# A graph attention kernel: ten of sixteen blocks per tile turned by DMA, the adjacency loaded in quarters

## The chip, the cores and the metric

One Trainium2 chip, one of its cores. The time is device microseconds for one execution of the whole program. TensorE is written PE, VectorE DVE, ScalarE ACT, GpSimd POOL, SyncE SP.

## What is computed

```python
h = jnp.maximum(_layernorm(x, axis=-1), 0.0)              # x: 8192 x 128, fp32
scores = jnp.einsum('nd,md->nm', h, ks)                   # ks: 8192 x 128, fp32
scores = leaky_relu(scores, negative_slope=0.2)
scores = jnp.where(adj > 0, scores, NEG_BIG)              # adj: 8192 x 8192, int32
attn = softmax(scores, axis=1)
out = x + jnp.einsum('nm,md->nd', attn, ks)
```

## The kernel before

The rows of x are taken in 64 tiles of 128. For a tile, its 8192 keys are worked in 16 blocks of 512 columns; two blocks are a pair, and two pairs (2048 columns) are a load of the adjacency.

- PE makes a block's scores from three fp16 products of 512 columns (h and the keys are each split in a high and a low half).
- DVE makes a mask from a load of the adjacency (L578), and adds it to a pair's scores (L596), which go from PSUM to SBUF with their running minimum. L611 takes the tile's minimum, once per tile.
- ACT does the leaky step (L458) and the exponentials (L467), a pair at a time, in place.
- The output product needs the probabilities transposed, 128 keys to the partition, in a high and a low fp16 half. There are two ways. A block of `BY_PE` is transposed by PE in fp32 (L376, four transposes) into PSUM; ACT then writes the high half (L475) and DVE the low half (L605). A block of `BY_DMA` is split first, by POOL (`split_half`: CAST at L317, subtraction at L319), and then both halves are turned at once by a DMA transpose (`turn`, L254, "turned block").
- PE adds either kind into the output with eight products per block (L391, L392).

Room for turned blocks: six slots for the halves (`R_SLOTS`), eight for the turned ones (`D_SLOTS`), both carved out of the buffer `keys_in` after the keys are done with. In the trace both appear as `keys_in`.

The order of all work is written out by hand. `steps` runs one step per tile, each of 16 slots `j`, and every engine's program has its own loop over these slots. In step i, PE makes the scores of tile i+1 while the rest works on tile i. A lag says how many slots after the block's own number a piece stands: `behind(i, j, lag, kind, ...)` gives the block of slot j - lag, if it is of that kind. On PE a turned block is added ten slots behind its number (`ADD_LAG`), a block of PE's own is transposed four and added six slots behind.

SP issues all DMAs in one queue, in the order of the program: a load of x and a store of the output for every four tiles, the adjacency loads (`load_adj`), and the turns. A turn waits for its split (`half_lo_ready`), so what stands behind it on SP waits too. A load waits until the mask that last read its slot is made (`mask_ready`). POOL's split waits for the exponentials and until the halves' slot was turned (`turned_in`, six turned blocks back). DVE's L596 waits until the pair of twelve pairs ago was transposed or split.

Of the kernel before, what the change touches and what calls it, by code (L numbers as in the profile page):

```python
# [5 lines left out]
def gat_kernel(nc: bass.Bass, x: bass.AP, adj: bass.AP, ks: bass.AP, out: bass.AP):  # L6
# [18 lines left out]
    PER_PAIR = PAIR // P  # L25
    LOAD = 2 * PAIR
    LOADS = M // LOAD
    SLOTS = 4
    ADJ_SLOTS = 4
    RING = 12  # L30
# [5 lines left out]
    EXP_LAG = 2  # L36
    T_LAG = 4
    OUT_LAG = 6
    LO_LAG = 3
    TURN_LAG = 5  # L40
    ADD_LAG = 10

    BY_DMA = tuple(b for b in range(BLOCKS) if b % 2 == 1 or b in (12,))
    BY_PE = tuple(b for b in range(BLOCKS) if b not in BY_DMA)

    EPS = 1e-5
# [10 lines left out]
    with ExitStack() as ctx:  # L57
# [6 lines left out]
        def sem(name):  # L64
            return ctx.enter_context(nc.semaphore(name))
# [49 lines left out]
        ps_out = psum("ps_out", [P, 2, BLOCK], fp32)  # L115


        adj_loaded = [sem(f"adj_loaded{s}") for s in range(2 * ADJ_SLOTS)]
        keys_loaded = [sem(f"keys_loaded{p}") for p in range(PAIRS)]
        x_loaded = [sem(f"x_loaded{s}") for s in range(2)]  # L120
        stored = sem("stored")
# [50 lines left out]
        def cols(b):  # L172
            return slice(b * BLOCK, (b + 1) * BLOCK)
# [54 lines left out]
        def _(sp):  # L228
# [8 lines left out]
                sp.wait_ge(out_ready, (g + 1) * GROUP)  # L237
                sp.dma_start(out_groups[g], out_tile[:, g % 2, :, :]).then_inc(stored, 16)

            def load_adj(q, p):  # L240
                n = q * PAIRS + p
                if n >= 2 * ADJ_SLOTS:
                    sp.wait_ge(mask_ready, n // 2 - ADJ_SLOTS + 1)
                sp.dma_start(adj_in[:, n // 2 % ADJ_SLOTS, n % 2 * PAIR:(n % 2 + 1) * PAIR],
                             adj_tiles[q // GROUP, q % GROUP, :, p * PAIR:(p + 1) * PAIR]).then_inc(adj_loaded[n % (2 * ADJ_SLOTS)], 16)

            def turn(t, b):
                n = nth_dma(t, b)
# [9 lines left out]
            for p in range(PAIRS):  # L258
                c = slice(p * PER_PAIR, (p + 1) * PER_PAIR)
                sp.dma_start(keys_in[:, c, :], key_chunks[:, c, :]).then_inc(keys_loaded[p], 16)  # L260
            for p in range(6):
                load_adj(0, p)
            load_x(1)

            def step(i, odd, more, this, prev, ahead):
                for j in range(BLOCKS):
                    if j % 2 == 1:
                        q, p = divmod((i + 1) * PAIRS + j // 2 + 6, PAIRS)
                        if q < TILES:
                            load_adj(q, p)  # L270
                    for b in (0, 1):
                        turning = behind(i, j, TURN_LAG - b, BY_DMA, this, prev) if j % 2 == 1 else None
                        if turning:
                            turn(*turning)
                    if j == 11 and prev and i % GROUP == 0:
                        store(i // GROUP - 1)
                        if i // GROUP + 1 < GROUPS:
                            load_x(i // GROUP + 1)
# [5 lines left out]
        def _(pool):  # L284
# [38 lines left out]

            def step(i, odd, more, this, prev, ahead):
                for j in range(BLOCKS):
                    for b in (0, 1):
                        split = behind(i, j, LO_LAG - b, BY_DMA, this, prev) if j % 2 == 1 else None
                        if split:
                            split_half(*split)
                    if j == 7 and ahead:  # L330
                        normalise(i + 2)

# [173 lines left out]
        def _(dve):  # L506
# [64 lines left out]
            def make_mask(q, k):  # L571

                n = q * LOADS + k
                dve.wait_ge(adj_loaded[2 * (n % ADJ_SLOTS)], (n // ADJ_SLOTS + 1) * 16)
                dve.wait_ge(adj_loaded[2 * (n % ADJ_SLOTS) + 1], (n // ADJ_SLOTS + 1) * 16)
                if q > 0 or k >= 2:
                    dve.wait_ge(masked_ready, q * PAIRS + 2 * k - 2)
                nc.vector.tensor_scalar(mask[:, k % 2, :], adj_in[:, n % ADJ_SLOTS, :], 0, MASKED, ALU.is_le, ALU.mult) \  # L578
                    .then_inc(mask_ready, 1)
# [125 lines left out]
```

## Time and profile before

| | |
|---|---|
| median of three runs | 1605.21 us (1602.86 to 1609.5) |
| the profiled execution's own time | 1603.36 us, span of its instructions 1601.6 us |
| granted TensorE clock | 0.996 |
| PE busy | 1561.6 us, 98% of the span |
| DVE, ACT, POOL busy | 89%, 84%, 83% |
| DMA | 434.52 MB, 271 GB/s over the span |

A line of the page or of an answer gives an engine, a source line, an operation, and its output and inputs by name, so `keys_in<-scores` at L317 is the split into the halves. "Busy" is time in which the engine has an instruction under way; PE's matmuls overlap, and their ends are modelled. SP has no busy time of its own: its rows (SPq) are the issue of a DMA, and a row's duration holds what the issue waited for as well. "To landing" is from the start of the issue until all of the DMA's completion signals are in.

### The profile page before, as it was taken

What the parts mean: (1) busy time and instruction counts of PE and PEld (TensorE: products, weight loads), DVE (VectorE), ACT (ScalarE), POOL (GpSimd) and SP (SyncE); (2) the same over time, 40 slices, a digit from 0 to 9 for tenths busy, and PEclk for the clock granted to TensorE, in tenths of its full rate; (3) what the DMA queues carried; (4) which work ended last, traced back from release to release, by engine and by line L of the source; (5) the groups of instructions that cost most, each with busy time, mean ns of one, the idle gap of its engine ahead of it and who ended that gap; (6) DMA issues with size and microseconds to landing.
All of it is one profiled execution on the core that took longest, in us unless ns stands there. A gap on an engine that the chain in (4) does not pass through costs nothing.

```text
span 1601.6 us, 37520 instructions
## 1 busy us (share of the span) xinstructions
PE 1561.6 (98%) x13186; PEld 1155.7 (72%) x13186; DVE 1423.2 (89%) x2528; ACT 1350.2 (84%) x2017; POOL 1332.6 (83%) x1352
## 2 busy tenths in 40 slices
PE   5699999999999999999999999999999999999998
PEld 3377777777777777777777777777777777777776
DVE  6998998998998998998898998899899899898895
ACT  6688888888888888888888888888888888888886
POOL 1588888888888888888888888888888888888887
PEclk9999999999999999999999999999999999999999
DMA  8699999999999999999999999999999999999996
GB/s 275 176 251 273 275 280 283 283 286 271 285 272 276 270 281 286 278 269 276 287 279 294 271 286 275 282 266 281 272 276 284 278 287 281 287 283 283 270 267 119
DMA packets 695098, 434.52 MB, mean 271 GB/s; under 512 B 617088, under 2 KB 625280, under 8 KB 694912
## 3 DMA queue, kind: packets, MB, share of 16 engines
q1 hardware_dynamic: 694912, 432.12, 111.2%
q8 instruction: 107, 1.75, 0.5%
q14 instruction: 79, 0.65, 0.1%
HBM read 276.82 MB, written 4.19 MB: 175 GB/s over the span
## 4 chain that ended last, share of the span: by engine, by line
PE 93%; DMA 1%; DVE 1%; POOL 1%; ACT 0%; issue 0%; POOLq 0%; DVEq 0%; ACTq 0%
PE ps_out L391 27%; PE ps_out L392 14%; PE ps_scores L365 13%; PE ps_scores L367 13%; PE ps_scores L366 13%; PE ps_T L376 12%; DMA keys_in<-keys_in 1%; PE ps_out L343 0%; PE ps_out L390 0%; POOL keys_in L319 0%; ACT scores L467 0%; DVE mask L578 0%; PE ps_out L389 0%; POOL keys_in L317 0%; DVE keys L567 0%
## 5 line engine op out<-in xcount | busy, mean ns | idle before, releaser
L319 POOL TENSOR_TENSOR keys_in<-scores,keys_in 128x512 f16<-128x512 f32 x576 | 728.8, 1265 | 46.5
L596 DVE CUSTOM_DVE_ANT_0 scores<-ps_scores,mask,minus_scale 128x1024 f32<-128x1024 f32 x512 | 653.8, 1277 | 17.0 <-PE ps_scores L367 2.1
L458 ACT ACTIVATE scores<-scores 128x1024 f32<-128x1024 f32 x512 | 537.6, 1050 | 79.5 <-DVE pair_min L596 79.5
L317 POOL CAST keys_in<-scores 128x512 f16<-128x512 f32 x576 | 463.7, 805 | 164.4 <-ACT scores L467 160.0
L467 ACT ACTIVATE scores<-scores,neg_max 128x1024 f32<-128x1024 f32 x512 | 583.1, 1139 | 0.0
L391 PE MATMUL ps_out<-keys,keys_in 128*128 128x256 f16 x2240 | 431.4, 273 | 1.1 <-DMA keys_in<-keys_in 1.1
L605 DVE TENSOR_TENSOR probsT_lo<-ps_T,probsT_hi 128x512 f16<-128x512 f32 x448 | 308.3, 688 | 126.9 <-ACT probsT_hi L475 118.1
L365 PE MATMUL ps_scores<-keysT_hi,hT_hi 128*128 128x512 f16 x1024 | 389.6, 381 | 17.2 <-DVE keysT_lo L560 10.6
L392 PE MATMUL ps_out<-keys,keys_in 128*128 128x128 f16 x2240 | 400.8, 219 | 0.0
L475 ACT ACTIVATE probsT_hi<-ps_T 128x512 f16<-128x512 f32 x448 | 264.7, 591 | 151.2 <-PE ps_T L376 146.8
L366 PE MATMUL ps_scores<-keysT_lo,hT_hi 128*128 128x512 f16 x1024 | 389.6, 380 | 0.0
L367 PE MATMUL ps_scores<-keysT_hi,hT_lo 128*128 128x512 f16 x1024 | 389.5, 380 | 0.0
L391 PE MATMUL ps_out<-keys,probsT_hi 128*128 128x256 f16 x1792 | 345.0, 273 | 8.2 <-issue 5.5
L578 DVE TENSOR_SCALAR mask<-adj_in 128x2048 bf16<-128x2048 int32 x256 | 326.1, 1274 | 0.0
L392 PE MATMUL ps_out<-keys,probsT_lo 128*128 128x128 f16 x1792 | 320.9, 220 | 0.0
L376 PEld LDWEIGHTS ps_T<-ident,scores 128*128 128x128 f32 x1792 | 224.1, 141 | 85.5 <-ACT scores L467 1.0
L391 PEld LDWEIGHTS ps_out<-keys,keys_in 128*128 128x128 f16 x2240 | 219.0, 98 | 81.0 <-DMA keys_in<-keys_in 2.6
L376 PE MATMUL ps_T<-ident,scores 128*128 128x128 f32 x1792 | 269.4, 273 | 0.5 <-ACT scores L467 0.5
L392 PEld LDWEIGHTS ps_out<-keys,keys_in 128*128 128x128 f16 x2240 | 219.0, 98 | 58.5
L391 PEld LDWEIGHTS ps_out<-keys,probsT_hi 128*128 128x128 f16 x1792 | 175.5, 98 | 32.8 <-issue 6.8
L367 PEld LDWEIGHTS ps_scores<-keysT_hi,hT_lo 128*128 128x128 f16 x1024 | 100.4, 98 | 121.7 <-issue 1.4
L392 PEld LDWEIGHTS ps_out<-keys,probsT_lo 128*128 128x128 f16 x1792 | 175.5, 98 | 11.5
(52 smaller groups left out, 829.5 us busy)
## 6 DMA issues: line engine op xcount, KB each, us to landing
adj_in<-in_adj_dram SPq DMA_DIRECT2D x512, 512.0 KB, 5.3
keys_in<-keys_in SPq DMA_TRANSPOSE x576, 5.5
x_in<-in_x_dram SPq DMA_DIRECT2D x16, 256.0 KB, 4.3
keys_in<-in_L_gnn_ks_dram SPq DMA_DIRECT2D x8, 512.0 KB, 7.4
out_dram<-out_tile SPq DMA_DIRECT2D x16, 256.0 KB, 3.8
```

What stands on the lines that cost most here:

```text
L317: nc.gpsimd.tensor_copy(half[:, 0:BLOCK], probs(t, b)).then_inc(half_hi_ready, 1)
L319: nc.gpsimd.tensor_tensor(half[:, BLOCK:2 * BLOCK], probs(t, b), half[:, 0:BLOCK], ALU.subtract) \
L365: nc.tensor.matmul(dst, hT_hi[:, odd, :], keysT_hi[:, cols(b)], start=True, stop=False)
L366: nc.tensor.matmul(dst, hT_hi[:, odd, :], keysT_lo[:, cols(b)], start=False, stop=False)
L367: nc.tensor.matmul(dst, hT_lo[:, odd, :], keysT_hi[:, cols(b)], start=False, stop=True) \
L376: mm = nc.tensor.transpose(ps_T[:, n % 2, k * P:(k + 1) * P], probs(t, b)[:, k * P:(k + 1) * P], ident[:, :])
L391: nc.tensor.matmul(o[:, 0:2 * D], hi_part, keys[:, c, :], start=(b == FIRST and k == 0), stop=False)
L392: return nc.tensor.matmul(o[:, D:2 * D], lo_part, keys[:, c, D:2 * D], start=False, stop=False)
L458: nc.scalar.activation(s, s, ACT.Prelu, alpha=1.0 / SLOPE).then_inc(leaky_ready, 1)
L467: nc.scalar.activation(s, s, ACT.Exp, bias=neg_max[:, t % 2:t % 2 + 1], scale=-SLOPE, accum_out=pair_sum[:, t % 2, p:p + 1]).then_inc(prob ...
L578: nc.vector.tensor_scalar(mask[:, k % 2, :], adj_in[:, n % ADJ_SLOTS, :], 0, MASKED, ALU.is_le, ALU.mult) \
L596: nc.vector.tensor_tensor_reduce(out=score_pair(q, p), in0=ps_scores[:, slots, :].rearrange("p s k -> p (s k)"), in1=mask[:, (p // 2) % 2, ...
```

## The change

Block 4 joins the blocks turned by DMA, so there are ten of them in a tile (1, 3, 4, 5, 7, 9, 11, 12, 13, 15) and six transposed by PE. The adjacency is loaded 512 columns (256 KB) at a time in place of 1024 (512 KB), one load in every slot in place of one in every second slot; a mask still covers 2048 columns, and waits for four loads. The splits and turns stood in odd slots only, up to two in a slot; now each stands in the slot of its own block number plus 2 (`LO_LAG`) and plus 4 (`TURN_LAG`), at most one in a slot.

```diff
     LOADS = M // LOAD
+    PER_LOAD = LOAD // BLOCK
...
-    LO_LAG = 3
-    TURN_LAG = 5
+    LO_LAG = 2
+    TURN_LAG = 4
     ADD_LAG = 10
 
-    BY_DMA = tuple(b for b in range(BLOCKS) if b % 2 == 1 or b in (12,))
+    BY_DMA = tuple(b for b in range(BLOCKS) if b % 2 == 1 or b in (4, 12))
...
-            def load_adj(q, p):
-                n = q * PAIRS + p
-                if n >= 2 * ADJ_SLOTS:
-                    sp.wait_ge(mask_ready, n // 2 - ADJ_SLOTS + 1)
-                sp.dma_start(adj_in[:, n // 2 % ADJ_SLOTS, n % 2 * PAIR:(n % 2 + 1) * PAIR],
-                             adj_tiles[q // GROUP, q % GROUP, :, p * PAIR:(p + 1) * PAIR]).then_inc(adj_loaded[n % (2 * ADJ_SLOTS)], 16)
+            def load_adj(q, b):
+                n = q * BLOCKS + b
+                if n >= PER_LOAD * ADJ_SLOTS:
+                    sp.wait_ge(mask_ready, n // PER_LOAD - ADJ_SLOTS + 1)
+                sp.dma_start(adj_in[:, n // PER_LOAD % ADJ_SLOTS, n % PER_LOAD * BLOCK:(n % PER_LOAD + 1) * BLOCK],
+                             adj_tiles[q // GROUP, q % GROUP, :, cols(b)]) \
+                    .then_inc(adj_loaded[n % (PER_LOAD * ADJ_SLOTS)], 16)
...
-            for p in range(6):
-                load_adj(0, p)
+            for b in range(12):
+                load_adj(0, b)
...
                 for j in range(BLOCKS):
-                    if j % 2 == 1:
-                        q, p = divmod((i + 1) * PAIRS + j // 2 + 6, PAIRS)
-                        if q < TILES:
-                            load_adj(q, p)
-                    for b in (0, 1):
-                        turning = behind(i, j, TURN_LAG - b, BY_DMA, this, prev) if j % 2 == 1 else None
-                        if turning:
-                            turn(*turning)
+                    q, b = divmod((i + 1) * BLOCKS + j + 11, BLOCKS)
+                    if q < TILES and (i, j) > (-1, 0):
+                        load_adj(q, b)
+                    turning = behind(i, j, TURN_LAG, BY_DMA, this, prev)
+                    if turning:
+                        turn(*turning)
...
                 for j in range(BLOCKS):
-                    for b in (0, 1):
-                        split = behind(i, j, LO_LAG - b, BY_DMA, this, prev) if j % 2 == 1 else None
-                        if split:
-                            split_half(*split)
+                    split = behind(i, j, LO_LAG, BY_DMA, this, prev)
+                    if split:
+                        split_half(*split)
...
-                dve.wait_ge(adj_loaded[2 * (n % ADJ_SLOTS)], (n // ADJ_SLOTS + 1) * 16)
-                dve.wait_ge(adj_loaded[2 * (n % ADJ_SLOTS) + 1], (n // ADJ_SLOTS + 1) * 16)
+                for s in range(PER_LOAD):
+                    dve.wait_ge(adj_loaded[PER_LOAD * (n % ADJ_SLOTS) + s], (n // ADJ_SLOTS + 1) * 16)
```

SP's queue before, in the middle of the program (a turn is a DMA_TRANSPOSE; its two halves are 8 x 128 columns):

```order
312 L254 DMA_TRANSPOSE keys_in<-keys_in 128x8x128
313 L244 DMA adj_in<-in_adj_dram 128x1024
314 L254 DMA_TRANSPOSE keys_in<-keys_in 128x8x128 x2
315 L244 DMA adj_in<-in_adj_dram 128x1024
316 L254 DMA_TRANSPOSE keys_in<-keys_in 128x8x128
```

SP's queue after the change, over a little more than half a tile:

```order
404 L256 DMA_TRANSPOSE keys_in<-keys_in 128x8x128
405 L245 DMA adj_in<-in_adj_dram 128x512 x2
406 L256 DMA_TRANSPOSE keys_in<-keys_in 128x8x128
407 L245 DMA adj_in<-in_adj_dram 128x512
408 L256 DMA_TRANSPOSE keys_in<-keys_in 128x8x128
409 L245 DMA adj_in<-in_adj_dram 128x512
410 L256 DMA_TRANSPOSE keys_in<-keys_in 128x8x128
411 L245 DMA adj_in<-in_adj_dram 128x512 x2
```

Where each turn had one load between it and the next, and two turns stood together once in a tile, there are now two loads of half the size at six places of a tile and one at four; no two turns stand together.

PE's order before, in slot 8, from the three products of a score block on (`ps_T` is the transpose's PSUM buffer, `ps_out` the output's):

```order
1551 L365 MATMUL ps_scores<-keysT_hi,hT_hi 128x512
1552 L366 MATMUL ps_scores<-keysT_lo,hT_hi 128x512
1553 L367 MATMUL ps_scores<-keysT_hi,hT_lo 128x512
1554 L376 MATMUL ps_T<-ident,scores 128x128 x4
1555 L391 MATMUL ps_out<-keys,probsT_hi 128x256
```

And after, in the same slot (its lines stand one higher in the file):

```order
1543 L364 MATMUL ps_scores<-keysT_hi,hT_hi 128x512
1544 L365 MATMUL ps_scores<-keysT_lo,hT_hi 128x512
1545 L366 MATMUL ps_scores<-keysT_hi,hT_lo 128x512
1546 L390 MATMUL ps_out<-keys,probsT_hi 128x256
1547 L391 MATMUL ps_out<-keys,probsT_lo 128x128
```

The four transposes of block 4 are gone; its output products move from slot 10 to slot 14, among those of the turned blocks.

## Rows read from the trace of the kernel before

**Rows 1.** The page's first part, busy time by engine

```profile
PE 1561.6 (98%) x13186; PEld 1155.7 (72%) x13186; DVE 1423.2 (89%) x2528; ACT 1350.2 (84%) x2017; POOL 1332.6 (83%) x1352
```

**Rows 2.** The page's chain that ended last, shares by engine and by line

```profile
PE 93%; DMA 1%; DVE 1%; POOL 1%; ACT 0%; issue 0%; POOLq 0%; DVEq 0%; ACTq 0%
PE ps_out L391 27%; PE ps_out L392 14%; PE ps_scores L365 13%; PE ps_scores L367 13%; PE ps_scores L366 13%; PE ps_T L376 12%; DMA keys_in<-keys_in 1%; PE ps_out L343 0%; PE ps_out L390 0%; POOL keys_in L319 0%; ACT scores L467 0%; DVE mask L578 0%; PE ps_out L389 0%; POOL keys_in L317 0%; DVE keys L567 0%
```

**Rows 3.** Timeline of DVE, 780 to 833: start us, us, instruction

```profile
781.71 0.16 DVE L611 TENSOR_REDUCE row_min<-pair_min 128x1 f32<-128x8 f32 x1
...
805.85 0.16 DVE L611 TENSOR_REDUCE row_min<-pair_min 128x1 f32<-128x8 f32 x1
```

**Rows 4.** Windows: stretch, its us, busy us (instructions) by engine, PEclk, DMA share, GB/s

```profile
779.97:804.06 24.09, 24.09 (x206) 17.90 (x205) 21.67 (x40) 20.66 (x32) 20.76 (x22) 1.00 1.15 285
18.00:24.00 6.00, 1.58 (x10) 1.16 (x10) 4.66 (x12) 3.71 (x6) 0.00 (x0) 0.80 1.03 411
```

**Rows 5.** The chain from 801 to 802.2: start us, us, what

```profile
801.64 0.44 PE ps_T L376 x4
```

**Rows 6.** Timeline of POOL, 780 to 833

```profile
782.12 0.61 POOL L317 CAST keys_in<-scores 128x512 f16<-128x512 f32 x1
782.81 1.18 POOL L319 TENSOR_TENSOR keys_in<-scores,keys_in 128x512 f16<-128x512 f32 x1
783.96 0.61 POOL L317 CAST keys_in<-scores 128x512 f16<-128x512 f32 x1
```

**Rows 7.** Waits of POOL, 781.9 to 806: us in total, times, longest

```profile
POOL keys_in L317 <- ACT scores L467: 2.2, 3, 1.2
```

**Rows 8.** Timeline of all engines, 803 to 804

```profile
803.35 1.26 DVE L578 TENSOR_SCALAR mask<-adj_in 128x2048 bf16<-128x2048 int32 x1
...
803.48 1.60 POOL L317 CAST keys_in<-scores 128x512 f16<-128x512 f32 x1
```

**Rows 9.** Lines L254 and L244: duration ns min/median/max, first and last start

```profile
L254 SPq DMA_TRANSPOSE keys_in<-keys_in x576: 1231/1677/3927, 63.0 to 1594.4; - x192
...
DMA to landing us min/median/max: 3.0/5.5/8.8
...
L244 SPq DMA_DIRECT2D adj_in<-in_adj_dram x512: 328/572/2006, 13.0 to 1555.0; - x171
...
DMA to landing us min/median/max: 3.6/5.3/11.2
```

**Rows 10.** Timeline of SP, 438 to 460

```profile
446.43 1.23 SPq L254 DMA_TRANSPOSE keys_in<-keys_in  x1
447.71 0.57 SPq L244 DMA_DIRECT2D adj_in<-in_adj_dram  x1
448.38 1.57 SPq L254 DMA_TRANSPOSE keys_in<-keys_in  x1
...
453.52 2.87 SPq L254 DMA_TRANSPOSE keys_in<-keys_in  x1
```

**Rows 11.** Timeline of SP, 262 to 272

```profile
267.55 0.57 SPq L238 DMA_DIRECT2D out_dram<-out_tile  x1
268.17 0.42 SPq L234 DMA_DIRECT2D x_in<-in_x_dram  x1
268.64 0.45 SPq L244 DMA_DIRECT2D adj_in<-in_adj_dram  x1
```

**Rows 12.** Waits of SP: us in total, times, longest

```profile
SPq L254 <- POOL keys_in L319: 443.0, 371, 3.5
SPq L244 <- DVE mask L578: 47.2, 52, 9.3
```

**Rows 13.** Groups of POOL by line: xcount, busy us, mean ns, idle before

```profile
L305 POOL TENSOR_SCALAR x_norm<-x_in,mean_var,rstd 128x128 f32<-128x128 f32 x64 | 103.4, 1616 | 6.7
L300 POOL TENSOR_TENSOR rstd<-var_eps,minus_half 128x1 f32<-128x1 f32 x64 | 36.1, 564 | 5.3
L297 POOL TENSOR_SCALAR var_eps<-mean_var 128x1 f32<-128x1 f32 x64 | 14.1, 220 | 38.2 <-DVE mean_var L513 32.8
```

More of the change, by code:

```diff
@@ L115, in gat_kernel @@
         ps_out = psum("ps_out", [P, 2, BLOCK], fp32)
-        adj_loaded = [sem(f"adj_loaded{s}") for s in range(2 * ADJ_SLOTS)]
+        adj_loaded = [sem(f"adj_loaded{s}") for s in range(PER_LOAD * ADJ_SLOTS)]
         keys_loaded = [sem(f"keys_loaded{p}") for p in range(PAIRS)]
```

## The prediction

> **What bounds the kernel now.** The engine totals come first: PE is busy for 1561.6 of 1601.6 us [rows 1], which by itself proves little. The chain that ended last says more: 93% of it is PE: products for the output 41% of the span, the three products of a score block 39%, the fp32 transposes (L376) 12% [rows 2]. One line per tile, the reduction at L611, gives the beat: it runs at 781.71 and at 805.85, 24.1 us apart [rows 3]; 64 such beats are 1542 us, and the rest of the span is start and end. In one beat PE is busy for 24.09 of 24.09 us [rows 4]. So PE alone sets the time, and PE time taken out of a beat comes out of the span, as long as the others keep the shorter beat. How near they are to that is the question of this case.
>
> **PE.** One more block turned by DMA takes four transposes of L376 out of each tile. On the chain they hold 0.44 us together [rows 5]. Its twelve score products and eight output products stay. New PE beat: 24.1 - 0.44 = 23.65 us. Over 64 tiles that would be 28 us. ACT and DVE each lose one block's piece and are idle for 10 to 14% of the beat [rows 1, 4]; nothing is due from them.
>
> **POOL.** It gets a tenth split per tile. Starts follow each other as 782.12, 782.81, 783.96 [rows 6]: 0.69 and 1.15, so 1.84 us for a block. In the beat shown POOL waits 2.2 us for the exponentials of ACT and for nothing else that is listed [rows 7], so its work, short gaps included, is 24.1 - 2.2 = 21.9 us, and 21.9 + 1.84 = 23.7 us after. That is the new PE beat and no less. The masks are in this already: the CAST at 803.48 takes 1.60 us and not 0.61, because the mask at L578 (1.26 us from 803.35) runs beside it [rows 8]. POOL can hold 23.7, but no longer catches up after anything.
>
> **SP.** This is the term I trust most and it goes the wrong way. SP is one queue that issues loads and turns in order, and an issue takes its sequencer time. A turn takes 1231 ns at least, and a load that follows a turn 572 ns at the median [rows 9]. With the short gaps between starts (446.43, 447.71, 448.38) a turn holds SP for 1.28 and the load behind it for 0.67 us [rows 10]. What does a load of half the bytes cost? A store of 256 KB behind a turn took 0.57 us (at 267.55), the same as a 512 KB load behind a turn, and the x load and the adjacency load behind it 0.42 and 0.45 us [rows 11]. So an issue's price is not in its bytes: a quarter load behind a turn costs 0.67 us, and one behind another load some 0.50 (0.45 and the gap, as from 268.17 to 268.64 and on).
> - Before: nine turns and eight loads, 9 x 1.28 + 8 x 0.67 = 16.9 us, with the store and the x load of every fourth tile (about 1 us in four) 17.1 us of 24.1.
> - After: ten turns, ten loads behind a turn and six behind a load (the order of the built program: double loads at six places, single ones at four). 10 x 1.28 + 10 x 0.67 + 6 x 0.50 + 0.25 = 22.75 us.
> So the floor of SP rises by 5.6 us, from 71% of the beat to 96% of the new one.
>
> That floor is without push-back. The turns' median is 1677 ns, 0.45 above their least [rows 9]. Only part of it is waiting for a split: 371 of 576 turns waited for one, and 205 did not [rows 12]; turns of 1.57 and 2.87 us stand beside ones of 1.23 [rows 10]. So a turn is also held until the DMA queue takes it. At what rate is the queue asked? SP's floor before offered 786 KB (a load and a turn) per 1.95 us, 400 GB/s, where the DMA engines moved 285 [rows 4] in a mix, and 411 in a stretch of loads alone [rows 4]. After, SP's floor offers 16 x 262 + 10 x 262 KB = 6.8 MB in 22.75 us, 300 GB/s. The queue is asked much less hard, so less push-back is due; not none, since 300 is still above the mean moved now. Bounds: 0 and 0.45 us per turn. I take 0.18, two fifths of what the median turn has now, since the asked rate comes down most of the way to the moved one. Ten turns: 1.8 us. **SP's beat: 22.75 + 1.8 = 24.5 us**, and that is above the 24.1 of today: (24.5 - 24.1) x 64 = +26 us.
>
> What hid SP until now: 443 us in total of waiting for the split, 47 us for a mask to free its slot [rows 12], 7.7 us per tile. The change spends 5.6 us of it, the shorter beat 0.45, and what is left must cover the push-back.
>
> Late next: a turned block has six slots, about 9 us, from its turn's place to its output products; a turn lands 5.5 us after its issue at the median, 8.8 at most [rows 9]. About 3.5 us are to spare, so single late turns cost nothing, but a queue slower than the beat uses that up within a few tiles and then PE waits at L391 for the turned block in every tile. Queued behind a late turn on SP are the adjacency loads; these are issued eleven blocks ahead and land 5.3 us after issue, so DVE's masks stay fed.
>
> **Bytes and the DMA engines.** The turned bytes grow from 9 x 262 to 10 x 262 KB per tile, the adjacency stays 4.2 MB: 6.55 to 6.8 MB, in 23.65 us 288 GB/s against 285 now [rows 4]. The pieces of the loads shrink from 4096 to 2048 bytes; x loads have such pieces, and no row shows them alone. If they moved at the 411 GB/s of the larger ones, the DMA engines would have room; a loss of a few per cent of rate would not.
> The Trainium skill (DMA: Bandwidth & Descriptors, Rules for kernel authors) asks for at least 1 MiB per DMA for most of the bandwidth, which speaks against cutting 512 KB loads in two. Its fit in the same page (2.0 us and the bytes at 436 GB/s per DMA) would give 16 x 2.6 = 42 us of loads per tile if they went one at a time. Here three or so are under way at once: a load lands 5.3 us after its issue [rows 9], and 17 DMAs start in 24.1 us, one per 1.4 us. So by the rows I price the smaller size at nothing beyond the issue.
>
> **The start.** Twelve issues instead of six before x's second load: 6 x 0.48 us behind a queue that is already filled with the keys; nothing.
>
> **Rivals.**
> - *SP keeps up; PE or POOL sets the beat.* If push-back falls to under 0.1 us per turn, SP needs under 23.7 us and the beat is 23.65 to 23.7: -0.4 x 64 = -26 to -28 us, 1577 to 1580. For it: the asked rate falls by a quarter, and the change spreads turns to at most one per slot where one slot had two. Against: the margin is 0.9 us per tile, POOL has none, and a turn waits for its split in order, so SP can't use its free moments ahead of time. Chance 0.25. The Trainium skill (DMA: Bandwidth & Descriptors, Issuing engines are not separate DMA queues) calls the sequencer's time to initiate a DMA usually small relative to the DMA itself; by that rule eight more issues would not count and this rival would be the forecast. Here the issue of a turn has at least 1.23 us against 3.0 to land at the least [rows 9], so it does count.
> - *Both effects cancel*, SP's beat at 24.0 to 24.2: 1598 to 1612. Chance 0.17.
> - *SP-bound as worked out*, 24.2 to 25.3: 1613 to 1682. Chance 0.48.
> - *Push-back stays as it is or POOL's lateness joins in.* At 0.36 to 0.45 us per turn SP's beat is 26.4 to 27.2 us: +2.3 to +3.1 x 64, 1750 to 1800. Or POOL's run of three splits in a row (blocks 3, 4, 5 and 11, 12, 13) with the normalisation behind block 5 (0.22 + 0.56 + 1.62 us, [rows 13]), 3 x 1.84 + 2.4 = 7.9 us in three slots of 1.5, makes the splits late by some 2 us and eats the turn's spare time. Chance 0.10 together.
> That the change doesn't do what it says is excluded by the order of the built program.
>
> **The numbers.** Sum against the profiled execution's own time, 1603.4: 1603.4 + 26 = 1629; the median of the runs shown stands 0.1% higher, so 1631. The range takes in PE's beat at the low end and an SP beat of 25.3 at the high end: 1577 to 1680. The likeliest case's own range is 1613 to 1680. A measurement of this kernel can tell about 0.5% from no change: faster than 1597 0.25, within 0.17, slower than 1613 0.58.
>
> **What the changed profile would show.** L611 24.4 to 24.6 us apart; L376 x1536; turns x640 and loads x1024 of 256 KB; SP's wait for POOL L319 down from 443 us to under 100; PE or its weight loads waiting at the turned L391 for the DMA, some 50 us where they now have under 4; loads' issue at 0.57 and 0.45 us as before. Wrong would be: the beat at 23.65 with SP still waiting over 100 us for splits (push-back gone), a quarter load's issue clearly under 0.45, or PE held by DVE's L596, which waits for splits that POOL finishes late.

## The result, and the profile after

The changed kernel takes 1665.81 us (median of 4 runs, 1658.7 to 1671.5) against 1604.03 us before (median of 4, 1602.62 to 1609.5): a ratio of 1.0381, 95% interval 1.0365 to 1.0397. That is 62 us slower; the forecast was 26. The profiled execution has a span of 1664.7 us and a granted clock of 0.998, so TensorE's clock has no part in it.

The page's first part after the change, busy time by engine, and its chain that ended last, by engine (beside [rows 1, 2]):

```profile
PE 1554.4 (93%) x12930; PEld 1112.0 (67%) x12930; DVE 1417.7 (85%) x2464; ACT 1329.6 (80%) x1953; POOL 1436.7 (86%) x1480
...
POOL 26%; PE 16%; DMA 14%; ACT 7%; DVE 7%; issue 6%; SPq 4%; POOLq 0%; DVEq 0%; ACTq 0%
```

PE was 93% of the chain and is 16% of it. Its place is taken by what the view reads as a loop: split on POOL, turn by DMA, product on PE. Whether POOL belongs in it is looked at below.

Three beats in the windows view (columns as in [rows 4]), from one row minimum at 763.31 to the third behind it at 837.92:

```profile
763.31:837.92 74.61, 70.97 (x601) 51.46 (x599) 65.11 (x115) 60.67 (x91) 66.58 (x69) 1.00 1.17 277
```

The same for three beats of the kernel before:

```profile
781.71:854.10 72.39, 72.39 (x617) 53.80 (x616) 65.23 (x118) 62.06 (x94) 62.41 (x64) 1.00 1.15 288
```

PE has less work (23.66 us a beat against 24.13) and now idles 1.2 us a beat; the beat is 24.87 here. Over the whole run the row minimum, this time by its line, with durations in ns and the first and last start:

```profile
L610 DVE TENSOR_REDUCE row_min<-pair_min x64: 160/161/163, 51.2 to 1637.3; 128x1 f32<-128x8 f32 x64
```

(1637.3 - 51.2) / 63 = 25.18 us a beat. Before it is (1575.6 - 50.5) / 63 = 24.21 us, from the same view of that kernel. The difference, 0.97 x 63 = 61 us, is the whole loss: it lies in the steady state, not at the ends.

What PE waits for, and what SP waits for, from the two views of waits (us in total, times, longest):

```profile
PE ps_out L390 <- DMA keys_in<-keys_in: 67.0, 93, 2.2
...
SPq L256 <- POOL keys_in L319: 261.5, 306, 3.7
```

PE's products of turned blocks (now L390) wait 67 us for the DMA. The weight loads of the same line wait 145 us. These overlap, and neither was over 4 us before. SP's listed wait for splits went from 443 us [rows 12] to 261.5. That looks as if SP still had four microseconds a beat to spare, and it had none, as its timeline shows over one beat (start us, us, instruction; x2 joins two issues in one row):

```profile
805.58 1.24 SPq L256 DMA_TRANSPOSE keys_in<-keys_in  x1
806.87 1.77 SPq L245 DMA_DIRECT2D adj_in<-in_adj_dram  x2
808.73 1.24 SPq L256 DMA_TRANSPOSE keys_in<-keys_in  x1
810.01 1.07 SPq L245 DMA_DIRECT2D adj_in<-in_adj_dram  x2
811.19 1.24 SPq L256 DMA_TRANSPOSE keys_in<-keys_in  x1
812.47 1.38 SPq L245 DMA_DIRECT2D adj_in<-in_adj_dram  x2
813.95 1.24 SPq L256 DMA_TRANSPOSE keys_in<-keys_in  x1
815.23 0.58 SPq L245 DMA_DIRECT2D adj_in<-in_adj_dram  x1
815.91 1.44 SPq L256 DMA_TRANSPOSE keys_in<-keys_in  x1
817.40 0.58 SPq L245 DMA_DIRECT2D adj_in<-in_adj_dram  x1
818.07 1.24 SPq L256 DMA_TRANSPOSE keys_in<-keys_in  x1
819.36 1.06 SPq L245 DMA_DIRECT2D adj_in<-in_adj_dram  x2
820.51 1.24 SPq L256 DMA_TRANSPOSE keys_in<-keys_in  x1
821.80 1.89 SPq L245 DMA_DIRECT2D adj_in<-in_adj_dram  x2
823.78 1.24 SPq L256 DMA_TRANSPOSE keys_in<-keys_in  x1
825.06 1.06 SPq L245 DMA_DIRECT2D adj_in<-in_adj_dram  x2
826.22 1.90 SPq L256 DMA_TRANSPOSE keys_in<-keys_in  x1
828.17 0.58 SPq L245 DMA_DIRECT2D adj_in<-in_adj_dram  x1
828.85 1.37 SPq L256 DMA_TRANSPOSE keys_in<-keys_in  x1
830.26 0.58 SPq L245 DMA_DIRECT2D adj_in<-in_adj_dram  x1
830.94 1.24 SPq L256 DMA_TRANSPOSE keys_in<-keys_in  x1
```

Ten turns from 805.58 to 830.94, 25.36 us, with no gap over 0.12 us. Turns that are taken at once cost 1.24, a pair of loads 1.06, a single load 0.58. At these prices the beat would be 12.4 + 6 x 1.06 + 4 x 0.58 + 1.4 of gaps = 22.5 us. What is over that is holding: 1.0 us on the turns (815.91, 826.22, 828.85), 1.9 us on pairs of loads (806.87, 812.47, 821.80).

Where is the wait for splits in this? POOL's subtractions, each the end of a split, from the same stretch:

```profile
819.66 1.17 POOL L319 TENSOR_TENSOR keys_in<-scores,keys_in 128x512 f16<-128x512 f32 x1
821.46 1.16 POOL L319 TENSOR_TENSOR keys_in<-scores,keys_in 128x512 f16<-128x512 f32 x1
823.25 1.16 POOL L319 TENSOR_TENSOR keys_in<-scores,keys_in 128x512 f16<-128x512 f32 x1
```

Splits and turns are made in the same order, so the n-th of one belongs to the n-th of the other. By that count these are the splits of blocks 3, 4 and 5, whose turns start at 826.22, 828.85 and 830.94: each split had been ready for 5.4 to 6.5 us. Counted so for all turns, none starts before its own split has ended, in either kernel. So a wait for a split stands in the gap ahead of a turn's row and not in the row's duration, and what a turn's row has over its least is holding. SP was in truth idle for its own split for 79.8 us before the change (118 turns) and for 6.2 us after (11 turns, all in the last 31 us), where the view lists 443.0 and 261.5: it puts down any stretch in which some later split's signal came. The same count over 56 tiles (from the fifth row minimum to the 61st), in us a beat:

| | before | after | `nine_quarter` | `ten_half` | `ten_whole` | `ten_quarter_hi` |
|---|---|---|---|---|---|---|
| beat | 24.10 | 25.16 | 24.14 | 25.91 | 27.43 | 24.24 |
| turns at their least | 11.08 | 12.31 | 11.08 | 12.26 | 12.31 | 11.91 |
| holding on turns | 5.67 | 1.51 | 2.00 | 6.78 | 11.21 | 1.08 |
| loads, x and stores | 5.06 | 9.51 | 9.08 | 5.40 | 2.70 | 9.07 |
| gaps | 2.26 | 1.82 | 1.99 | 1.45 | 1.23 | 2.18 |
| of these, waiting for the turn's own split | 0.90 | 0.00 | 0.24 | 0.00 | 0.00 | 0.42 |

(The four kernels on the right belong to the experiments below.) Before the change SP waited for splits 0.9 us a beat; a tenth turn needs 1.28 of issue alone.

### The profile page after: what moved, and what is told of

The parts are those of the page before. It is cut to its first block, busy times and chain, and to the rows that moved or that the text cites. A ratio compares the mean times of both kernels' runs of the same rounds, so it can differ in the third digit from the quotient of the medians.

```text
span 1664.7 us, 37777 instructions
## 1 busy us (share of the span) xinstructions
PE 1554.4 (93%) x12930; PEld 1112.0 (67%) x12930; DVE 1417.7 (85%) x2464; ACT 1329.6 (80%) x1953; POOL 1436.7 (86%) x1480
## 4 chain that ended last, share of the span: by engine, by line
POOL 26%; PE 16%; DMA 14%; ACT 7%; DVE 7%; issue 6%; SPq 4%; POOLq 0%; DVEq 0%; ACTq 0%
DMA keys_in<-keys_in 14%; POOL keys_in L319 14%; POOL keys_in L317 9%; PE ps_out L390 5%; ACT scores L466 4%; DVE mask L577 3%; DVE scores L595 2%; ACT scores L457 2%; PE ps_out L391 2%; PE ps_scores L366 2%; PE ps_scores L365 2%; PE ps_scores L364 2%; PE ps_T L375 2%; POOL var_eps L297 2%; SPq L256 2%
## 5 line engine op out<-in xcount | busy, mean ns | idle before, releaser
L319 POOL TENSOR_TENSOR keys_in<-scores,keys_in 128x512 f16<-128x512 f32 x640 | 795.3, 1243 | 51.6
L317 POOL CAST keys_in<-scores 128x512 f16<-128x512 f32 x640 | 511.6, 799 | 118.5 <-ACT scores L466 117.2
L390 PE MATMUL ps_out<-keys,keys_in 128*128 128x256 f16 x2496 | 482.0, 273 | 68.6 <-DMA keys_in<-keys_in 67.0
L391 PE MATMUL ps_out<-keys,keys_in 128*128 128x128 f16 x2496 | 446.3, 219 | 0.0
L604 DVE TENSOR_TENSOR probsT_lo<-ps_T,probsT_hi 128x512 f16<-128x512 f32 x384 | 263.6, 686 | 175.5 <-ACT probsT_hi L474 174.6
L390 PEld LDWEIGHTS ps_out<-keys,keys_in 128*128 128x128 f16 x2496 | 243.7, 98 | 206.2 <-DMA keys_in<-keys_in 145.4
L577 DVE TENSOR_SCALAR mask<-adj_in 128x2048 bf16<-128x2048 int32 x256 | 364.4, 1424 | 0.1
L390 PE MATMUL ps_out<-keys,probsT_hi 128*128 128x256 f16 x1536 | 294.7, 273 | 9.4 <-issue 6.5
L391 PE MATMUL ps_out<-keys,probsT_lo 128*128 128x128 f16 x1536 | 274.1, 219 | 0.0
L391 PEld LDWEIGHTS ps_out<-keys,keys_in 128*128 128x128 f16 x2496 | 244.3, 98 | 38.5
L375 PE MATMUL ps_T<-ident,scores 128*128 128x128 f32 x1536 | 230.5, 273 | 0.5 <-ACT scores L466 0.5
L390 PEld LDWEIGHTS ps_out<-keys,probsT_hi 128*128 128x128 f16 x1536 | 150.2, 98 | 40.0 <-issue 9.4
```

What stands on the lines that cost most here:

```text
L317: nc.gpsimd.tensor_copy(half[:, 0:BLOCK], probs(t, b)).then_inc(half_hi_ready, 1)
L319: nc.gpsimd.tensor_tensor(half[:, BLOCK:2 * BLOCK], probs(t, b), half[:, 0:BLOCK], ALU.subtract) \
L375: mm = nc.tensor.transpose(ps_T[:, n % 2, k * P:(k + 1) * P], probs(t, b)[:, k * P:(k + 1) * P], ident[:, :])
L390: nc.tensor.matmul(o[:, 0:2 * D], hi_part, keys[:, c, :], start=(b == FIRST and k == 0), stop=False)
L391: return nc.tensor.matmul(o[:, D:2 * D], lo_part, keys[:, c, D:2 * D], start=False, stop=False)
```

## The experiments

Seventeen kernels ran, in the groups below. Unless said otherwise a ratio is against the kernel before, whose own median beside them was 1603.3 to 1604.0 us.

**Which part of the change costs.** `ten_half` is the changed kernel with the old 512 KB loads:

```diff
-                    q, b = divmod((i + 1) * BLOCKS + j + 11, BLOCKS)
-                    if q < TILES and (i, j) > (-1, 0):
-                        load_adj(q, b)
+                    if j % 2 == 1:
+                        q, p = divmod((i + 1) * PAIRS + j // 2 + 6, PAIRS)
+                        if q < TILES:
+                            load_adj(q, p)
```

> The changed kernel (ten turned blocks, one per slot) with the adjacency again in loads of 1024 columns, eight per tile. Theory A (SP's queue: issues plus the time a DMA is held fill 25.1 us of every beat): eight issues fewer take 8 x 0.55 = 4.4 us off SP's floor of 22.75, so SP is no longer full by issues, and the beat falls to between 23.7 (POOL) and 24.1: 1577 to 1605 us. Theory B (the tenth split on POOL sets the beat, the chain shows POOL first): the split is still there, so the time stays within 1% of 1666. Theory C (the 2048-byte pieces move more slowly): as A.

1710.68 us, ratio 1.0665 (1.0638 to 1.0693): slower than the change itself, as neither theory had it.

`nine_quarter` is the kernel before with quarter loads, placed as the change places them.

> The kernel before (nine turned blocks, its lags) with the adjacency in quarter loads, one per slot: the other half of the change alone. Theory A: SP's floor is 9 x 1.28 + 9 x 0.67 + 7 x 0.50 + 0.25 = 21.3 us, with the 2.4 us of holding seen after the change 23.7, just under PE's 24.1: 1603 to 1620 us. Theory B: as before, 1600 to 1608. Theory C: clearly slower than before, towards 1640 to 1665, since all the small pieces are there.

1605.08 us, 1.0005 (0.9995 to 1.0015): eight more issues a tile and pieces of 2,048 bytes cost the time of nine blocks nothing. SP pays 4.0 us a beat more for loads and gets 3.7 back in holding on turns (the table above).

`nine_cut32` cuts each 512 KB load of the kernel before into 992 and 32 columns, sixteen issues a tile. Half of the issues have pieces of 3,968 bytes, the other half of 128.

> The kernel before with each 1024-column load issued as two, one of 992 and one of 32 columns: eight issues more per tile, the same bytes, nearly all in pieces of 3968 bytes. Theory A: SP's floor rises from 17.1 to 21.1 us and what a turn is held stays near the 5.7 us per beat of before, so SP needs more than 24.1: 1620 to 1700 us. Theories B and C (the number of issues costs nothing): 1600 to 1610.

1616.99 us, 1.0071 (1.0048 to 1.0095). That is 13 us, between the two forecasts, and the even split in `nine_quarter` doesn't have it. Whether the issues or the 128-byte pieces cost it wasn't tested.

`nine_half_lags` takes the new lags alone, and `ten_half_oldlags` block 4 alone (`b in (4, 12)`, nothing else changed).

> The kernel before with the new lags alone (block 12's split and turn in slots of their own). All theories: PE's beat stays, 1600 to 1610 us.

> The kernel before with block 4 turned by DMA and nothing else changed: split and turn of block 4 stand with those of block 5 in one slot, as 12 and 13 do. Theory D: the queue has the same ten turns and eight loads as in ten_half, 1690 to 1730 us. If spreading the turns over the slots is what helps or harms, it differs from 1711 by more than 1%. Theory B: 1650 to 1720.

1603.37 us, 0.9997 (0.9988 to 1.0006), and 1699.61 us, 1.0588 (1.0568 to 1.0609). So the tenth turned block is the whole loss and more, +96 us. Both results lie where the queue's theory put them; the range of POOL's holds the second too. The lags cost nothing with nine blocks and 11 us with ten and 512 KB loads (1710.68 against 1699.61). The quarter loads, which my sum made the culprit, give 45 us back (1710.68 to 1665.81).

**What a turn waits for.** SP's timeline in `ten_half`, and behind it three single turns of that kernel by their line (duration ns; start; landing is counted from the start of the issue):

```profile
782.97 2.24 SPq L255 DMA_TRANSPOSE keys_in<-keys_in  x1
...
785.95 4.95 SPq L255 DMA_TRANSPOSE keys_in<-keys_in  x2
...
797.55 1.47 SPq L255 DMA_TRANSPOSE keys_in<-keys_in  x1
...
799.77 5.60 SPq L255 DMA_TRANSPOSE keys_in<-keys_in  x2
```

```profile
L255 SPq DMA_TRANSPOSE keys_in<-keys_in x1: 2238/2238/2238, 783.0 to 783.0; - x1
DMA to landing us min/median/max: 6.9/6.9/6.9
...
L255 SPq DMA_TRANSPOSE keys_in<-keys_in x1: 2902/2902/2902, 785.9 to 785.9; - x1
...
L255 SPq DMA_TRANSPOSE keys_in<-keys_in x1: 1465/1465/1465, 797.5 to 797.5; - x1
DMA to landing us min/median/max: 6.6/6.6/6.6
...
L255 SPq DMA_TRANSPOSE keys_in<-keys_in x1: 3462/3462/3462, 799.8 to 799.8; - x1
```

The turn of 782.97 lands at 789.9; the issue of the next one, from 785.95, is held for 2.90 us and ends at 788.85, 1.0 us before that. The turn of 797.55 lands at 804.15; the next one's issue ends at 799.77 + 3.46 = 803.23, 0.9 us before. The same in the changed kernel:

```profile
L256 SPq DMA_TRANSPOSE keys_in<-keys_in x1: 1237/1237/1237, 823.8 to 823.8; - x1
DMA to landing us min/median/max: 5.2/5.2/5.2
...
L256 SPq DMA_TRANSPOSE keys_in<-keys_in x1: 1902/1902/1902, 826.2 to 826.2; - x1
```

823.78 + 5.2 = 828.98, and the issue of the turn behind it ends at 826.22 + 1.90 = 828.12, 0.9 us before. These three are the common case, not a rule. Of the turns held by over 0.2 us with their split ready, 330 of 451 in `ten_half` end their issue 0.8 to 1.2 us before the turn ahead lands, and 71 of 112 in the changed kernel; but the turn of 782.97 above, held for 1.0 us, was let go 2.5 us before the one ahead of it landed, and in `ten_quarter_hi` (below) only 15 of 76 are in that band. Where turns are held, then, they mostly follow the landing of the turn ahead, and what stands in front of a turn counts: with 512 KB loads a turn lands in 5.4 us at the median, with quarter loads in 4.2 (the lines' own views).

**Size of the loads.** `ten_third` cuts each 2,048 columns into 688, 680 and 680, `ten_mixed` into 1,024, 512 and 512, both with twelve loads a tile in the same slots; `ten_whole` has 1 MB loads on SP.

```diff
-    PER_LOAD = LOAD // BLOCK
+    PER_LOAD = 3
+    CUTS = (0, 688, 1368, 2048)
```

> The changed kernel with three loads per mask (688, 680, 680 columns), twelve per tile, placed so that a turn mostly has one load ahead of it, twice two. Theory D: SP's issues need 10 x 1.28 + 10 x 0.67 + 2 x 0.50 + 0.25 = 20.75 us, and a turn behind one 350 KB load is held to about 0.15 us less than its issues take, so holding stays rare, 2.5 to 3.5 us per beat: 23.3 to 24.3, which POOL and PE keep at 23.7 or more: 1580 to 1615 us. That would be level with or faster than the kernel before. Theory B (POOL): 1650 to 1680.

> As ten_third, same twelve issues in the same places, but a mask's loads are 1024, 512 and 512 columns. If only the number of issues counts, the same time as ten_third within 0.5%. Theory D: the turns behind a 1024-column load (four per tile) are held 0.7 us or so more than there, the others a little less: 1.5 to 2.5 us per beat more, 1.5 to 8% over ten_third.

> Ten turned blocks, adjacency in whole loads of 2048 columns (1 MB, four per tile) on SP. Theory D (what the first four runs left: SP's queue is full in every kernel with ten blocks; a turn costs SP either its issue or, if that is longer, the time until about 1 us before the turn ahead of it has landed, and each load in between delays that landing by its bytes): SP's issues alone need 10 x 1.28 + 4 x 0.67 + 0.25 = 15.7 us, but four of the ten turns stand behind 1 MB, so they are held about 4 us each and the other six 1.3 to 2.3: 24 to 30 us, 1600 to 1960, most likely 1690 to 1760. Theory A as first put (issues alone): 1577 to 1605. Theory B (POOL's tenth split): 1650 to 1680, as after.

1657.67 us, 1.0346 (1.0321 to 1.0372); 1675.2 us, 1.0442 (1.0426 to 1.0457); 1806.3 us, 1.1263 (1.1246 to 1.128). The first missed what I expected by far: thirds are only 8 us better than quarters, and the intervals of the two ratios overlap. The second is 1.1% over the first, outside both forecasts (within 0.5%, and 1.5 to 8%). The third is slower than its likeliest range and inside the wide one. The size of the largest load matters at a fixed number of issues (1,024 columns against 688: 17.5 us), and below a third of 1 MB smaller loads give nothing more.

`ten_whole_act` moves 1 MB loads to ACT's queue so that they don't stand between turns, and `nine_whole_act` does so to the kernel before.

```diff
+                    if j % 4 == 1:
+                        n = ((i + 1) * BLOCKS + j + 11) * PARTS // 4
+                        if n < PARTS * LOADS * TILES:
+                            issue_adj(act, n)
```

> Ten turned blocks, whole loads, but issued by ACT's queue, so SP holds nothing but turns, x and stores. Theory D: no load stands between two turns in SP's queue, SP needs 12.8 us of issues; if a load on ACT's queue doesn't push a turn's landing far back, the beat falls to POOL's or PE's 23.7: 1575 to 1600 us, faster than both kernels. Theory B: 1650 to 1680, since POOL does the same splits. A turn that lands late because of the shared DMA engines would leave it above 1610 and show as PE waiting for the turned block.

> The kernel before with whole loads issued by ACT: the control for the issue on ACT. All theories: PE's beat of 24.1 stays, 1600 to 1610 us. Slower would show what four issues of 0.45 us per tile cost on ACT.

The first takes 2073 to 2210 us in four executions. The second takes 2060 to 2119; its ratio, of the two shortest, is 1.2883 (1.2839 to 1.2928), 462 us. Both missed by some 400 us or more, with granted clocks of 0.85 to 0.91. What four issues on ACT cost was thus not learnt; they themselves take 0.33 to 0.40 us each. SP is held: its issue of a turn takes up to 17.3 us and the slowest turn lands after 28.6. The DMA issues and the waits for turned blocks of `nine_whole_act`, from an execution of 2118.6 us:

```profile
adj_in<-in_adj_dram ACTq DMA_DIRECT2D x253, 1024.0 KB, 6.6
keys_in<-keys_in SPq DMA_TRANSPOSE x576, 6.6
...
PEld ps_out L395 <- DMA keys_in<-keys_in: 426.9, 105, 13.2
PE ps_out L395 <- DMA keys_in<-keys_in: 375.8, 96, 12.7
```

A turn lands in 6.6 us at the median and PE waits up to 13 us for one. Why a load that starts on another queue delays a turn so much was not settled.
The Trainium skill (DMA: Bandwidth & Descriptors, Issuing engines are not separate DMA queues) says that DMAs of all engines interleave on the same 16 DMA engines whoever issues them, and that a second issuer saves sequencer time alone; the trace agrees that nothing was won, and the loss of 462 us is more than the page leads one to expect.

**The queue taken off the path.** `ten_quarter_halfbytes` halves the bytes of each adjacency load after the first sixteen, so half the adjacency is stale. `ten_quarter_hi` turns only the high half of each block after the first eight; the low halves are stale.

```diff
-                sp.dma_start(turned[:, n % D_SLOTS, :, :], halves[:, n % R_SLOTS, :], transpose=True) \
+                k, w = (2 * PER_BLOCK, SLOT) if n < D_SLOTS else (PER_BLOCK, BLOCK)
+                sp.dma_start(turned[:, n % D_SLOTS, 0:k, :], halves[:, n % R_SLOTS, 0:w], transpose=True) \
```

> The changed kernel, in which every adjacency load after the first sixteen brings 256 of its 512 columns (the other half of the mask is left from earlier tiles): the same issues, half the adjacency's bytes. Theory A in its two parts: if the holding (2.4 us per beat) is the DMA engines' doing, it mostly goes, SP needs 22.8 to 23.5 and the beat is POOL's 23.7, 1575 to 1590 us; if it is the issue itself, nothing changes, 1655 to 1670. Theory B: within 1% of 1666. Theory C: much faster, since fewer bytes are moved, 1580 to 1610.

> The changed kernel, in which every turn after the first eight turns only the high halves (512 of 1024 columns; the low halves in the products are stale): the same number of issues and loads, half the turned bytes. Theory D: if a turn's issue goes by its size, 1.23 falls to 0.6 to 0.8 us and its landing comes earlier, SP needs 17 to 19 us, and the beat is POOL's or PE's 23.7: 1575 to 1590 us. If an issue has a price of its own whatever it moves, as the loads' has, SP stays at 22.75 plus less holding: 1600 to 1650. Theory B: 1650 to 1680.

1628.03 us, 1.0149 (1.0133 to 1.0164), and 1611.71 us, 1.0048 (1.0035 to 1.0062). Number and order of the issues are those of the change. The first result lies between all the forecasts for it, the second in that of an issue price that doesn't go by bytes. The turn's line in `ten_quarter_hi`:

```profile
L257 SPq DMA_TRANSPOSE keys_in<-keys_in x640: 1188/1195/2708, 62.9 to 1603.2; - x160
...
DMA to landing us min/median/max: 2.4/3.4/6.0
```

Half the bytes cost the same issue (1,195 ns against 1,237) and land in 3.4 us instead of 4.2. PE then waits 1.9 us in all for turned blocks, and 54 of the 62 us are gone. The issue time of SP, 22.5 us less 10 x 0.04, was never the bound by itself.

A rival to the queue stays open: the 16 DMA engines behind it. The page gives the time of the queue's packets as a share of the engines' span (packets, MB, share), after the change:

```profile
q1 hardware_dynamic: 836224, 448.94, 112.9%
```

It is 111.2% before, 100.6% in `ten_quarter_halfbytes` and 95.6% in `ten_quarter_hi`; counted over the middle of the run, 16 packets or more are under way for 94% of the time before, 95% after, and 65% in each of the two. The changed kernel moves 16.8 MB more than the one before, both at 271 GB/s, and 16.8 MB at that rate are 62 us. Bytes alone can't be the bound, since the same 451 MB take 1657.7 us in thirds and 1806.3 as whole loads (273 and 250 GB/s). But both kernels with half the bytes relieve the queue and the engines at once, and no run here relieves one without the other.

**The 28 us that didn't come.** PE's work is 0.44 us a beat shorter, yet `ten_quarter_hi` is 8 us slower than before. Its beat, and what PE waits for in it:

```profile
785.30:809.55 24.25, 23.81 (x204) 17.41 (x202) 22.81 (x39) 20.18 (x31) 22.47 (x24) 1.00 0.99 231
```

```profile
PE ps_out L391 <- DVE probsT_lo L605: 27.6, 63, 0.8
```

63 waits, one a tile, of 0.44 us: as much as the change saved. One step back, DVE's timeline around that wait and POOL's beside it:

```profile
801.47 2.13 DVE L578 TENSOR_SCALAR mask<-adj_in 128x2048 bf16<-128x2048 int32 x1
803.53 0.68 DVE L605 TENSOR_TENSOR probsT_lo<-ps_T,probsT_hi 128x512 f16<-128x512 f32 x1
```

```profile
801.36 1.16 POOL L320 TENSOR_TENSOR keys_in<-scores,keys_in 128x512 f16<-128x512 f32 x1
802.47 1.61 POOL L318 CAST keys_in<-scores 128x512 f16<-128x512 f32 x1
```

The mask takes 2.13 us where 1.22 is its least. It starts 0.11 us into a subtraction that runs to 802.52 and ends at 803.60, 1.08 us after it. The CAST behind the subtraction takes 1.61 us instead of 0.61 and ends at 804.08, 0.48 us after the mask. Each waits for the other. The probsT_lo behind the mask is late for PE.
The Trainium skill (SBUF — State Buffer, Who interferes with whom) calls the port pair that VectorE and GpSimd share "an exclusive lock" that a tensor_scalar can take and for which the later one blocks; these rows agree, in both directions.

Three kernels on top of `ten_quarter_hi` and one control test this. `ten_hi_halfmask` makes each mask of half its columns, `ten_hi_halfsplit` takes the difference in each split over half its columns, `ten_hi_halfbytes` halves the load bytes, and `nine_hi` is `nine_quarter` with high halves alone. Of these the first leaves half of each mask stale, the second a part of the low halves that no turn reads.

```diff
-                nc.gpsimd.tensor_tensor(half[:, BLOCK:2 * BLOCK], probs(t, b), half[:, 0:BLOCK], ALU.subtract) \
+                w = BLOCK if n < R_SLOTS else BLOCK // 2
+                nc.gpsimd.tensor_tensor(half[:, BLOCK:BLOCK + w], probs(t, b)[:, 0:w], half[:, 0:w], ALU.subtract) \
```

> The kernel that turns only high halves of ten blocks (1611.7 us), and each mask made of 1,024 of its 2,048 columns after the first two, so that its other half is stale and the output is not the reference's. Theory P (VectorE and GpSimd hold each other up: masks of 1,728 ns mean beside GpSimd's splits make probsT_lo late by 0.43 us a tile, and GpSimd is 98% taken): masks of 700 to 950 ns, splits that wait less for them, no wait of TensorE at the output products; 1,577 to 1,592 us. Rival Q (what is left of the loss is still the DMA queue or TensorE's own instructions): unchanged at 1,607 to 1,615 us.

> The same base (high halves alone, 1611.7 us), and the difference of each split taken over 256 of its 512 columns after the first four, which no turn reads here; the output is not the reference's. GpSimd loses some 10 x 0.5 us a tile, and VectorE's work stays. Theory P in its form 'GpSimd is full': 1,577 to 1,592 us, masks back near 1,300 to 1,500 ns. In its form 'the mask's place on VectorE is late whatever GpSimd does': 1,600 to 1,612. Rival Q: unchanged at 1,607 to 1,615 us.

> High halves alone and half the bytes of each adjacency load after the first sixteen (output not the reference's). Theory P: the DMA queue has already left the path, so nothing moves: 1,607 to 1,613 us. Rival Q (the queue still costs something): below 1,603 us.

> Nine blocks turned with the lags of before, quarter loads, and only the high halves turned (output not the reference's). Theory P: TensorE's own 24.1 us a tile bounds nine blocks, so 1,600 to 1,606 us as before. Rival (turned blocks cost nine blocks something as well): 1,575 to 1,597 us.

1583.89 us, 0.9871 (0.9853 to 0.989); 1582.48 us, 0.9863 (0.9847 to 0.9879); 1612.52 us, 1.005 (1.0037 to 1.0063); 1603.34 us, 0.9995 (0.9986 to 1.0004). Four hits for theory P: relief of either engine of the pair brings out most of PE's gain, relief of the queue does nothing more, and nine blocks never had the problem. Three beats of `ten_hi_halfsplit`, and the masks of `ten_quarter_hi` and of `ten_hi_halfsplit` by their groups (busy us, mean ns, idle before):

```profile
770.60:841.70 71.10, 71.08 (x604) 52.23 (x603) 63.25 (x114) 61.12 (x90) 52.87 (x70) 1.00 1.01 238
```

```profile
L578 DVE TENSOR_SCALAR mask<-adj_in 128x2048 bf16<-128x2048 int32 x256 | 442.4, 1728 | 0.1
```

```profile
L579 DVE TENSOR_SCALAR mask<-adj_in 128x2048 bf16<-128x2048 int32 x256 | 321.8, 1257 | 0.1
```

71.10 / 3 = 23.70 us with PE busy throughout. The masks are back at 1,257 ns, even under the 1,300 expected, though nothing was done to them.

`ten_quarter_halfsplit` does the same to the changed kernel itself, with both halves turned (the rest of each low half is stale).

> The changed kernel with both halves turned, and the difference of each split taken over 256 of its 512 columns after the first four (the rest of each low half is stale; the output is not the reference's). GpSimd loses some 5 us of work a tile and all 640 turns, 1,024 loads and their bytes stay. Theory S (two bounds one under the other: VectorE and GpSimd at 24.25 us a tile, and over it the one queue of SP at 25.1): GpSimd's relief alone gains little, 1,650 to 1,666 us. Rival (late splits are what holds SP's queue and makes the turned blocks late, so that the two costs are one): 1,583 to 1,620 us.

1662.22 us, 1.0365 (1.0351 to 1.0379): POOL's busy time falls from 1436.7 to 1130.6 us, 4.8 us a beat, and the time falls by 4 us. The loss doesn't start with late splits, as their count above says too.

## Why the prediction was right in sign and short in size

The step that failed is the holding in SP's beat. The sum had 1.8 us of it, all on turns and none on loads; the runs show 1.5 on turns and 0.9 on loads, which is most of what separates the 26 us forecast from the 62 measured. That SP's queue would set the beat, above PE and POOL, was right, if the DMA engines behind it are taken with it.

The accounting that the runs give: PE's shorter work, -21 us (1603.3 to 1582.5, `ten_hi_halfsplit`); VectorE and GpSimd in each other's way, +29 (1582.5 to 1611.7); the queue with the DMA engines behind it, +54 (1611.7 to 1665.8). They lie under each other, not side by side: the second is hidden while the third holds the beat.

- *PE at 23.65 us a beat*: right. It is 23.66 us of busy time in the changed kernel and the beat of `ten_hi_halfsplit` is 23.70. Over the run 21 of the 28 us arrive. Of the other 7 some 6 are in five beats of 24.3 to 25.9 us, behind the first, among ones of 23.66; PE's products wait 6.6 us there for turned blocks, 10 times.
- *POOL at 23.7 us, "the masks are in this already"*: wrong. The 1.84 us of a split were priced without what a split costs DVE. With ten splits the mean mask goes from 1,274 to 1,424 ns in the changed kernel and to 1,728 in `ten_quarter_hi`, and the pair needs 24.25 us. The rival that SP keeps up, 1577 to 1580, was given 0.25, and its POOL at 23.7 doesn't hold: with the queue out of the way the kernel is at 1612.
- *SP's floor of 22.75 us*: right as a sum (22.5 in the timeline shown), issue prices unchanged as forecast. But its rise was read as the reason. `ten_half` has a floor of some 17.1 + 1.28 = 18.4 us by the same prices and a beat of (1682.9 - 50.9) / 63 = 25.9, longer than that of the change. Issue time alone doesn't set the beat. SP's beat is its issues and the holding together, and the holding grows with what stands before a turn.
- *Push-back, 0.18 us a turn and none on loads*: this is the term of the sum that was mis-sized. Over 56 tiles the turns have 1.51 us of it, 0.15 a turn, near the forecast. The loads have some 0.9 us over the prices of the timeline, for which the sum had nothing (the beat shown has 1.0 and 1.9). 22.75 + 1.5 + 0.9 = 25.15, the beat measured, against 24.5. So the loss a beat came out as 0.97 us over the run and not 0.4. That the turns' term comes out near is in part luck: its 0.45 us is a median with split waits thought to be in it, and the mean holding before was 5.67 / 9 = 0.63 us a turn.
- *"What hid SP until now: 443 us in total of waiting for the split"*: wrong, though no term of the sum comes from it. I read the waits as room that the new issues would use up first. Waiting for their own splits, turns stood 79.8 us, 0.9 us a beat in the middle of the run, and not 7; 118 of 576 turns waited so, and not 371. In `ten_half`, 107 us slower than before, the row stands at 510 us and the wait by count is 13. The row names the semaphore that came last, not what held SP. The two can be told apart by setting each turn's start beside the end of its own split.
- *"Twelve issues", "quarter loads raise the floor"*: `nine_quarter` at 1.0005 and `ten_half` at 1.0665 show that the quarter loads are the helpful half of the change. Of the floor's rise of 5.6 us the sum gave some 4.3 to the eight further loads; these were paid, and beside ten turns bought back more than that in holding (6.78 to 1.51 us a beat). So the sign was right for a reason that is only half the forecast's: the tenth turn costs, the loads don't.
- *PE waiting for the DMA, some 50 us*: 67. *SP's wait for splits under 100*: 261.5 in the view, 6.2 by count; the sign asked for the wrong number.

Open: why a held turn is mostly let go about 1 us before the turn ahead has landed, what holds the loads, whether the queue's order or the DMA engines set its pace, and why turns beside loads from another queue become so slow. No kernel tried here that computes all of the reference beats the kernel before.

## What to carry to other kernels

A queue that issues both large loads and transposes is read by the landing of each transpose against the issue of the next, not by adding issue times: change the size of what stands between them and see whether the beat moves. A wait that a profile puts down to a producer is room only if the consumer starts right after its own item is ready; the n-th start beside the n-th end tells. And work given to GpSimd has to be priced with what it does to VectorE's instructions on the shared port, most of all where VectorE feeds the engine that is meant to gain.

## What the runs showed of the hardware

- A transpose of 262 KB and one of 131 KB cost SP 1,237 and 1,195 ns of issue, and land in 4.2 and 3.4 us.
- A held transpose's issue ends 0.9 to 1.0 us before the transpose ahead has landed in the three pairs shown, and 0.8 to 1.2 us before in 330 of 451 with 512 KB loads (`ten_half`).
- The row of a transpose's issue doesn't hold its wait for a semaphore: none of 576 and 640 starts before its data is ready.
- With nine transposes a tile, where PE sets the time, 256 KB loads cost the kernel no more than 512 KB ones (1.0005); with ten, 1 MB loads are 95.6 us worse than 512 KB ones (1806.3 against 1710.7).
- Loads on a second queue beside transposes: 29% slower for the whole kernel, transposes up to 13 us late for PE.
- A mask of 1.22 us takes up to 2.2 us and a CAST of 0.61 us up to 1.6 us when VectorE and GpSimd meet.
